# Two layers of attention and a feed-forward: projections dealt out into the leads, and loads asked in another order

## The chip, the cores and the metric

One NeuronCore of one Trainium2 chip. The metric is the device time of one execution in microseconds (us), the median of several runs. Five engines work side by side, each through its own instructions in order, and wait for each other by counting semaphores: TensorE (PE in the profile; PEld is its weight loads) multiplies from SBUF into the eight banks of PSUM; ScalarE (ACT) and VectorE (DVE) read PSUM and SBUF; GpSimd (POOL) works on SBUF; SyncE (SP) issues most of the DMA transfers. An engine that waits keeps everything behind it in its own queue waiting, the DMAs that it is to issue included.

## The reference

All in float32. `x` is (2, 512, 320), `ctx` is (2, 1024, 192).

```
# layer 0: 8 heads of 40
enc, ca = ctx[:, :-4], ctx[:, -4:]
hs   = mha(x @ Wq, enc @ Wk, enc @ Wv)                  # 512 queries, 1020 keys
q1   = einsum('btc,th->bch', ca, Wq_ca)[:, indices]     # 192 rows, repeated to 512
hs1  = mha(q1, x, x)                                    # 512 keys
hs2  = mha(hs1 @ Wq, ca @ Wk_ca, ca @ Wv_ca)            # 4 keys
x    = (hs + hs2) @ Wout + b_out + x
# layer 1: 20 heads of 16
h1 = ln(x); x = attn(h1, h1,  q1, k1, v1, o1_w, o1_b) + x   # self: 512 keys
h2 = ln(x); x = attn(h2, ctx, q2, k2, v2, o2_w, o2_b) + x   # cross: 1024 keys
h3 = ln(x); a, g = split(h3 @ ff_w1 + ff_b1)
out = (a * gelu(g)) @ ff_w2 + ff_b2 + x
```

## The kernel before, in words

**Numbers.** Matmuls run on a reduced-precision float type (fp32r). Where float32 is wanted, an operand is split into a high part (a cast by ScalarE) and a low part (the difference, by VectorE, in join phases by GpSimd), and a product is the sum of high by high, high by low and low by high. A feature tile is 128, 128 or 64 of the 320 features (`FTILES`), held on partitions. Of the last tile both parts share 128 partitions ("mixed"). The class `Prepared` (L407) holds these splits of inputs: `first_in` for the first layer, `self_in`, `cross_in` for the second; its semaphore `low` counts the parts in a fixed order.

**Projections** (`Projection`, L466) are lists of jobs. A job of kind "s" makes one feature tile of queries or keys: a group of matmuls into one of a few PSUM banks, ScalarE's copy into the high half of one of four slots of the tile `split` (the ring), VectorE's subtraction into the low half, SyncE's store of both to a DRAM scratch (`q0_d`, `k0_d`, `q1_d`, ...). A slot may be filled again when its store has landed (semaphores `stored`); a bank when VectorE is done with it (`low`). A job of kind "v" makes the values of 128 tokens: five or eight matmuls of 320 columns into one of two banks, copied by ScalarE. Kinds "k" and "w" make small products for the image tokens (`ca`), with small matmuls. `first` (L506) has the queries and keys of batch 0 and the values of both batches of layer 0; `second` (L507) the rest of layer 0 and the keys and values of cross attention; `selfp` and `selfv` the queries and keys, and the values, of self attention; `crossp` the queries of cross attention.

**Attention** (`Stream`, `Attention`). A group is two heads (layer 0) or four (layer 1) of a batch. SyncE loads a group's keys and queries from the scratch into one of four slots (`k_sl`, `q_sl`; `sp_load` L706: four DMAs a group in layer 0, eight in layer 1). Each group is passed twice. In the first pass ("items", `item` L805) TensorE makes scores with queries on partitions, 512 keys an item, into the banks 4, 5 and 6 in turn, and VectorE takes each item's maximum (`reduce` L966, line L974, one instruction an item). When a group is done (`part_maxima` L949), its negated maxima are split in two parts, turned by TensorE (`flip` L820), copied by ScalarE (`flipped`) and sent by a DMA into two more rows of the queries (`sp_load_m` L696). In the second pass the scores come out with keys on partitions and the maximum already subtracted (`scores` L841), ScalarE takes the exponential (L938), and `values` (L857) multiplies by the values into bank 7.
Items are counted in chunks: two items a chunk in layer 0, four in layer 1, one chunk per step of the second pass. The first pass runs ahead of the second by `lead` chunks: 13 in the first attention, 8 in self, 12 in cross. So each attention opens with a lead in which there is only the first pass; then steps of both. `first` attention and cross attention have two items per row of scores (1020 and 1024 keys), self has one. In the first attention's lead the jobs of `second` are dealt out over the 13 chunks by count (`share` L510), after the items of each chunk; `probs`, where the exponentials go, lies on the ring, so ScalarE waits for all stores before the first exponential.

**The front.** SyncE issues the loads "a" (x of batch 0, Wq), "c" (context of batch 0, Wk, Wv), "e" (context of batch 1). GpSimd clears some tiles and, when the nine low parts of `first` are done, issues "d" (weights of the image tokens, Wout, a mask) and "f" (x of batch 1, k2, v2, the identity, small tensors): eleven DMAs. The engines run `first`, split the remaining inputs, and start the first attention. SyncE loads group 0's slot after all stores of `first`, group 1's and 2's in the lead after the shares 0 and 4.

**Between the attentions** lie joins (`pe_join` L1205, `dve_join` L1251, `act_join` L1280): per token tile the output projection, residual, layer norm, a transpose, the split of the result. `early` (L1200) puts the first half of the next projection's jobs behind the last three token tiles, and the rest behind the join. Then come (self) `selfv`, the wait for all low parts, and the lead; (cross) the wait for all low parts, and the lead. In `sp_self` (L759) group 0 is loaded after eight stores and when six have landed; in `sp_cross` (L780) keys are loaded ahead, and the queries of group 0 after three stores have landed.

The feed-forward ends the kernel.

## Time and profile before

| | us |
|---|---|
| median of 3 runs (910.27 to 910.87) | 910.78 |
| profiled execution | 911.72 |
| its span | 909.9 |
| TensorE busy | 842.4 (93%) |
| VectorE busy | 605.4 (67%) |
| ScalarE busy | 474.5 (52%) |
| GpSimd busy | 101.7 (11%) |

A busy TensorE is not one at its peak: its granted clock is a column of its own in the windows (1.00 is 2.4 GHz, 0.50 is 1.2 GHz). The chain that ended last is 62% TensorE and 23% VectorE. All times of rows are microseconds from the start of the span.

### The profile page before, as it was taken

The numbers are of one execution on the slowest core, as the hardware profiler recorded it, in microseconds if no ns is written. First come the engines' busy times: TensorE is split into PE (matmuls) and PEld (weight loads), VectorE is DVE, ScalarE is ACT, GpSimd is POOL, SyncE is SP. The second block draws the span as 40 slices with busy tenths as digits, with TensorE's granted clock in tenths as the row PEclk, the third lists the DMA queues.
The fourth block names the chain that finished last, engine by engine and source line by source line (L and its number), as shares of the span: only waits on it lengthen the run. The fifth ranks groups of instructions, "written<-read, shape, count | busy, mean of one in ns | idle before, by whom it ended". The sixth has DMA issues, their size and how long they took to land.

```text
span 909.9 us, 11416 instructions
## 1 busy us (share of the span) xinstructions
PE 842.4 (93%) x4148; PEld 461.6 (51%) x4148; DVE 605.4 (67%) x1147; ACT 474.5 (52%) x706; POOL 101.7 (11%) x142
## 2 busy tenths in 40 slices
PE   4759989999999999999998989999999999899998
PEld 3647644444457577433333643333333332578988
DVE  4245547777685343889994688999999991866241
ACT  4523344545543352366677704776766779575030
POOL 3200000500004142000001610000000000130000
PEclk9968999999997999589999956999999999999999
DMA  6938658733212047122207230222232000600000
GB/s 222 275 104 239 205 155 282 199 85 110 65 57 66 1 134 222 59 71 68 66 11 128 71 127 1 54 54 54 53 54 53 1 1 2 246 0 1 30 1 30
DMA packets 30967, 83.18 MB, mean 91 GB/s; under 512 B 5173, under 2 KB 9213, under 8 KB 28607
## 3 DMA queue, kind: packets, MB, share of 16 engines
q1 hardware_dynamic: 30110, 79.71, 30.9%
q0 software_dynamic: 800, 2.73, 1.0%
q8 instruction: 33, 0.54, 0.3%
q14 instruction: 24, 0.19, 0.1%
HBM read 56.12 MB, written 25.89 MB: 90 GB/s over the span
## 4 chain that ended last, share of the span: by engine, by line
PE 62%; DVE 23%; DMA 7%; ACT 3%; issue 3%; POOL 1%; SPq 0%; ACTq 0%; DVEq 0%; POOLq 0%
PE PS L872 17%; PE PS L815 13%; DVE maxp L974 10%; PE PS L1408 8%; PE PS L566 7%; PE PS L852 6%; DVE negm L974 5%; PE PS L1426 4%; PE PS L1213 3%; DMA k_d<-split 2%; DMA ca_nat<-in_ca 2%; DVE turned L1007 1%; DMA q_sl<-msplit 1%; ACT probs L938 1%; DMA w_v<-in_Wv 1%
## 5 line engine op out<-in xcount | busy, mean ns | idle before, releaser
L938 ACT ACTIVATE probs<-PS 128x1024 f32<-128x1024 f32 (+1 forms) x336 | 311.7, 972 | 149.9 <-PE PS L852 144.4
L974 DVE TENSOR_REDUCE maxp<-PS 128x1 f32<-128x512 f32 x448 | 280.1, 679 | 44.6 <-PE PS L815 43.6
L815 PE MATMUL PS<-k_sl,q_sl 48*128 48x512 f32 (+3 forms) x640 | 262.4, 489 | 24.1 <-DMA q_sl<-q_d 11.2
L815 PEld LDWEIGHTS PS<-k_sl,q_sl 48*128 48x128 f32 (+2 forms) x640 | 119.3, 199 | 200.8 <-DVE maxp L974 120.5
L852 PE MATMUL PS<-q_sl,k_sl 50*128 50x512 f32 (+3 forms) x672 | 203.2, 433 | 8.3 <-ACT probs L938 5.2
L974 DVE TENSOR_REDUCE negm<-PS 128x1 f32<-128x512 f32 (+1 forms) x192 | 120.9, 679 | 29.4 <-PE PS L815 29.3
L852 PEld LDWEIGHTS PS<-q_sl,k_sl 50*128 50x128 f32 (+2 forms) x672 | 102.7, 191 | 56.0 <-ACT probs L938 24.4
L872 PE MATMUL PS<-probs,v2c 128*32 128x512 f32 x640 | 86.6, 610 | 1.0
L604 DVE TENSOR_TENSOR split<-PS,split 128x512 fp32r<-128x512 f32 (+3 forms) x54 | 34.9, 650 | 53.7 <-ACT split L581 53.7
L872 PE MATMUL PS<-probs,v0c 128*64 128x512 f32 (+1 forms) x256 | 62.8, 612 | 0.0
L581 ACT CAST split<-PS 128x512 fp32r<-128x512 f32 (+3 forms) x54 | 29.8, 554 | 52.8 <-PE PS L566 41.4
L1039 POOL TENSOR_TENSOR packed<-turned,recip 128x256 f32<-128x256 f32 x20 | 12.7, 635 | 372.2 <-DVE recip L1010 372.2
L1408 PE MATMUL PS<-act_high,w_high 128*128 128x512 f32 x120 | 48.0, 400 | 3.8 <-DVE w_low L1384 2.5
L1007 DVE STREAM_TRANSPOSE turned<-PS 128x512 f32<-128x512 f32 (+1 forms) x36 | 22.9, 637 | 40.6 <-PE PS L872 40.0
L872 PE MATMUL PS<-probs,v1c 128*32 128x512 f32 x320 | 45.6, 639 | 2.1 <-DVE turned L1007 1.2
L1408 PE MATMUL PS<-act_high,w_low 128*128 128x512 f32 x120 | 47.3, 394 | 0.0
L922 ACT CAST msplit<-PS 32x128 fp32r<-32x128 f32 (+2 forms) x36 | 9.0, 249 | 72.6 <-PE PS L826 72.6
L1285 ACT ACTIVATE act_t<-PS,params 128x128 f32<-128x128 f32 x72 | 27.8, 457 | 17.3 <-PE PS L1231 17.3
L1408 PE MATMUL PS<-act_low,w_high 128*128 128x512 f32 x80 | 31.6, 396 | 0.0
L566 PE MATMUL PS<-x_high,w_q_high 128*128 128x512 f32 (+1 forms) x42 | 14.8, 449 | 17.1 <-DVE w_s_low L427 12.2
L872 PEld LDWEIGHTS PS<-probs,v0c 128*64 128x64 f32 (+1 forms) x256 | 15.7, 138 | 28.6 <-issue 25.6
L1469 DVE SCALAR_TENSOR_TENSOR ff_raw<-PS,params,gelu 128x512 f32<-128x512 f32 x20 | 15.0, 750 | 20.8 <-ACT gelu L1449 20.8
(182 smaller groups left out, 1012.8 us busy)
## 6 DMA issues: line engine op xcount, KB each, us to landing
k_d<-split SPq DMA_DIRECT2D x20, 512.0 KB, 3.6
q_d<-split SPq DMA_DIRECT2D x12, 512.0 KB, 3.1
k_sl<-k_d SPq DMA_DIRECT2D x8, 640.0 KB
k_sl<-k_d SPq DMA_DIRECT2D x40, 128.0 KB
q_sl<-q_d SPq DMA_DIRECT2D x40, 128.0 KB
k_sl<-k_d SPq DMA_DIRECT2D x20, 256.0 KB
w_raw<-in_ff_w SPq DMA_DIRECT2D x1, 3840.0 KB, 11.6
k_d<-split SPq DMA_DIRECT2D x10, 256.0 KB, 3.4
```

The costliest lines, as they stand in the source:

```text
L566: mm = nc.tensor.matmul(o, w, a, start=(k == 0), stop=(k == len(j["mm"]) - 1))
L581: nc.scalar.copy(split[0:j["m"], i % RING, 0, 0:j["n"]], split_bank(ph, j)).then_inc(ph.high, 1)
L604: nc.vector.tensor_tensor(split[0:j["m"], i % RING, 1, 0:j["n"]], split_bank(ph, j), split[0:j["m"], i % RING, 0, 0:j["n"]].bitcast(F32), ...
L815: nc.tensor.matmul(PS[0:a.qt, SBANKS[k % 3], 0:cn], q_view(g)[f:f + a.rows, j // a.stack, q * a.qt:(q + 1) * a.qt], k_view(g)[f:f + a.rows ...
L852: mm = nc.tensor.matmul(PS[0:sz, 2 * (x % 2) + half, 0:a.nq], k_view(g)[f:f + a.rows + 2, j // a.stack, t * 128:t * 128 + sz], q_view(g)[f ...
L872: mm = nc.tensor.matmul(PS[w * j:w * j + w, OBANK, 0:a.nq], a.vc[0:sz, tile, a.vw * h:a.vw * h + w], probs[0:sz, x % PRING, half, 0:a.nq], ...
L938: nc.scalar.activation(probs[0:a.size[t], x % PRING, :, 0:a.nq], PS[0:a.size[t], 2 * (x % 2):2 * (x % 2) + 2, 0:a.nq], ACT.Exp, scale=a.sc ...
L974: nc.vector.tensor_reduce((maxp if nch > 1 else negm)[0:a.qt, g.turn, o:o + 1], PS[0:a.qt, SBANKS[k % 3], 0:a.chunks[c][1]], AX.X, ALU.max ...
L1007: nc.vector.transpose(turned[:, 0:a.nq], PS[:, OBANK, 0:a.nq]).then_inc(st.out_read, 1)
L1285: o = nc.scalar.activation(act_t[0:fn, m, t * 128:(t + 1) * 128], PS[0:fn, 4 + t % 2, 128 * m:128 * m + 128], ACT.Identity, bias=params[0: ...
L1408: mm = nc.tensor.matmul(PS[:, up_bank(i, part), :], w[:, k, f0:f0 + 128], a[:, k, cols], start=(n == 0), stop=(n == len(UP_TERMS) - 1))
L1426: mm = nc.tensor.matmul(PS[:, 4 + t % 4, 0:D], a[:, m, rows], w[:, m, :], start=(m == 0 and n == 0), stop=(m == FT - 1 and n == 2))
```

## The change

1. **The front.** "a" is split: x has its own semaphore and Wq ("q") another, so that x is cast when it is there. x and the context are split by feature tiles (`x0a`, `x0b`, `c1a`, ...). Keys are made tile by tile (both halves of the 1024 keys of a tile in turn), and ScalarE and VectorE split the context of batch 1 between key jobs. The values of batch 1 go from `first` to `second`. `second` begins with the keys of batch 1; its jobs name the inputs that they need, and the splits of x of batch 1, k2 and v2 stand in front of single jobs; the small products of the image tokens are dealt out among the others. Group 0's slot load is issued after seven stores, when five have landed. GpSimd issues x of batch 1 when "c" has landed, and "f" and "d" when group 0's slot has been loaded.
2. **Self attention.** After the join only the first six jobs of `selfp` are made; the other six and the eight of `selfv` are dealt out over seven of the lead's eight chunks. In both leads with jobs, a chunk's jobs now stand before its items. `selfp` has three banks. Slot loads stand between the stores.
3. **Cross attention.** In the lead a chunk's four items go to banks 0 to 3 or 4 to 7, and VectorE takes all four maxima in one instruction. The queries of group 0 are loaded after one store.

The diff, cut to its core:

```diff
     loads = {
-        "a": [(act_t[:, :, 0:SQ], ins["x_t"][:, :, 0:SQ]), (w_s0[:], ins["Wq"])],
+        "a": [(act_t[:, :, 0:SQ], ins["x_t"][:, :, 0:SQ])],
+        "q": [(w_s0[:], ins["Wq"])],
...
+        "x": [(act_t[:, :, SQ:TOK], ins["x_t"][:, :, SQ:TOK])],
+        "f": [(w_k2[:], ins["k2"]), (w_v2[:], ins["v2"]),
...
     def first_jobs():
-        return q0_jobs(0) + key_jobs(WK0, k0_d, 0) + value_jobs(WV0, 0, v0c, 0) + value_jobs(WV0, 0, v0c, 1)
+        return q0_jobs(0) + key_jobs(WK0, k0_d, 0) + value_jobs(WV0, 0, v0c, 0)
 
     def second_jobs():
+        q_jobs, k_jobs = q0_jobs(1), key_jobs(WK0, k0_d, 1)
+        k_jobs[0]["needs"] = ("c1a", "c1b")
+        k_jobs[2].update(prepare=("x1a",), prepare_loaded=(loaded_x1, ALL_X1))
+        k_jobs[4].update(prepare=("x1b",), prepare_loaded=(loaded_x1, ALL_X1))
+        q_jobs[0]["needs"] = ("x1a", "x1b")
+        q_jobs[0].update(prepare=("wk2",), prepare_loaded=(loaded_f, ALL_F))
+        q_jobs[1].update(prepare=("wv2",), prepare_loaded=(loaded_f, ALL_F))
...
+        ca_jobs[0]["loaded"] = (loaded_f, ALL_F)
...
+        split_jobs = k_jobs + q_jobs
+        for i, j in enumerate(k2_jobs):
+            split_jobs += [j] if i % 2 == 0 else [j, ca_jobs[i // 2]]
...
+        ca_rows[0]["loaded"] = (loaded_d, ALL_D)
...
+        whole_jobs = value_jobs(WV0, 0, v0c, 1) + v2_jobs[:2] + ca_rows[:1] + v2_jobs[2:4] + ca_rows[1:]
+        whole_jobs += v2_jobs[4:9] + ca_outs[:1] + v2_jobs[9:12] + ca_outs[1:] + v2_jobs[12:]
...
     first = Projection("first", first_jobs())
-    second = Projection("second", second_jobs(), (0, 1, 2), (3, OBANK))
-    selfp = Projection("selfp", self_jobs(), (2, 3, 6, 7))
+    second = Projection("second", second_jobs(), (0, 1, 2), (3, OBANK), first)
+    selfp = Projection("selfp", self_jobs(), (2, 3, OBANK))
...
+    class Side:
...
+        def share(self, x):
+
+            n = len(self.jobs)
+            return self.jobs[min(x, self.span) * n // self.span:min(x + 1, self.span) * n // self.span]
+
+    def alternate(ph, jobs, other, others):
+
+        out = []
+        for i, j in enumerate(jobs):
+            out += [(ph, j)] + ([(other, others[i // 2])] if i % 2 else [])
+        return out + [(other, j) for j in others[len(jobs) // 2:]]
+
+    first_side = Side([(second, j) for j in second.jobs], A_MAIN.lead)
+    self_side = Side(alternate(selfp, selfp.jobs[2 * KF:], selfv, selfv.jobs), A_SELF.lead - 1)
...
     def sp_first(sp):
         st = S_FIRST
-        first.wait_stored(sp)
+        sp_projection(sp, first, first.jobs[:Q0_END + 4])
         sp.wait_ge(first_ones, 1)
+        first.wait_some_stored(sp, Q0_END + 2)
         sp_load(sp, st, 0)
+        sp_projection(sp, first, first.jobs[Q0_END + 4:])
         for x in range(A_MAIN.kt + 1):
-            sp_projection(sp, second, share(second, x, st.lead))
+            sp_projection(sp, second, [j for _, j in first_side.share(x)])
+            if x == 0:
+                first.wait_stored(sp)
             if x in (0, 4):
                 sp_load(sp, st, 1 + x // 4)
...
     def sp_self(sp):
         st = S_SELF
-        sp_projection(sp, selfp, selfp.jobs[:2 * KF + 2])
+        sp_projection(sp, selfp, selfp.jobs[:4])
         sp.wait_ge(stack_ones, 1)
-        selfp.wait_some_stored(sp, 2 * KF)
+        selfp.wait_some_stored(sp, 2)
         sp_load(sp, st, 0)
-        sp_projection(sp, selfp, selfp.jobs[2 * KF + 2:])
-        for i in range(1, SLOTS - 1):
-            sp_load(sp, st, i)
+        sp_projection(sp, selfp, selfp.jobs[4:2 * KF])
+        sp_load(sp, st, 1)
+        sp_projection(sp, selfp, selfp.jobs[2 * KF:2 * KF + 4])
+        selfp.wait_some_stored(sp, 4)
+        sp_load(sp, st, 2)
+        sp_projection(sp, selfp, selfp.jobs[2 * KF + 4:])
+        sp_load_m(sp, st, 0)
+        selfp.wait_stored(sp)
         sp.dma_start(w_s0[:], ins["q2"]).then_inc(loaded_q2, 16)
...
     def sp_cross(sp):
...
-        sp_projection(sp, crossp, crossp.jobs[:KF])
+        sp_projection(sp, crossp, crossp.jobs[:1])
+        crossp.wait_some_stored(sp, 1)
+        sp_load_q(sp, st.groups[0])
+        sp_projection(sp, crossp, crossp.jobs[1:KF])
...
+        def wide_items(c):
+            per = st.groups[0].a.per_step
+            if c >= 2:
+                pe.wait_ge(st.score_free, per * (c - 1))
+            for n, (i, m) in enumerate(st.chunk(c)[1]):
...
+                nc.tensor.matmul(PS[0:a.qt, wide_bank(c) + n, 0:cn],
...
+            if st.chunk(c)[0] is not None:
+                pe.wait_ge(st.score_free, per * c)
+                flip(st.chunk(c)[0], waits=False)
...
         for x in range(st.lead):
-            maxima([x])
-            if side is not None:
-                pe_projection(pe, side, share(side, x, st.lead))
-            flips([x])
...
+            if wide:
+                wide_items(x)
+            else:
+                if side is not None:
+                    for ph, j in side.share(x):
+                        pe_projection(pe, ph, [j])
+                maxima([x])
+                flips([x])
+        if wide:
+            pe.wait_ge(st.score_free, st.groups[0].a.per_step * (st.lead - 1 + st.lead % 2))
...
+        def wide_maxima(c):
...
+            dve.wait_ge(st.score, st.item_at[i, m] + a.per_step)
+            to = maxp[0:a.qt, g.turn, :].rearrange("p (e r c) -> p r c e", e=a.stack, c=2)[:, t, :, :]
+            nc.vector.tensor_reduce(to, PS[0:a.qt, wide_bank(c):wide_bank(c) + 4, :].rearrange(
+                "p (c e) n -> p c e n", e=a.stack), AX.X, ALU.max).then_inc(st.score_free, a.per_step)
...
@@ VectorE's program @@
-            first_in.dve(dve, "c0", "wk0", "wv0")
-            dve_projection(dve, first, first.jobs[:K0_END])
+            first_in.dve(dve, "c0a", "c0b", "wk0", "wv0")
+            dve_projection(dve, first, first.jobs[:Q0_END + 3])
             dve.wait_ge(loaded_e, ALL_E)
-            first_in.dve(dve, "c1")
+            first_in.dve(dve, "c1a")
+            dve_projection(dve, first, first.jobs[Q0_END + 3:Q0_END + 5])
+            first_in.dve(dve, "c1b")
+            dve_projection(dve, first, first.jobs[Q0_END + 5:K0_END])
             dve.wait_ge(loaded_f, ALL_F)
-            first_in.dve(dve, "x1", "wk2", "wv2")
             dve.wait_ge(loaded_d, ALL_D)
-            dve_attention(dve, S_FIRST, side=second)
+            dve_attention(dve, S_FIRST, side=first_side)
@@ GpSimd's program @@
             pool_rows_first(pool, range(SLOTS - 1), 1)
-            pool.wait_ge(first.low, first.ns)
+            pool.wait_ge(loaded_c, ALL_C)
+            for dst, part in loads["x"]:
+                pool.dma_start(dst, part).then_inc(loaded_x1, 16)
+            pool.wait_ge(q_loaded[S_FIRST.groups[0].place], S_FIRST.groups[0].loads)
+            for dst, part in loads["f"]:
+                pool.dma_start(dst, part).then_inc(loaded_f, 16)
             for dst, part in loads["d"]:
                 pool.dma_start(dst, part).then_inc(loaded_d, 16)
-            for dst, part in loads["f"]:
-                pool.dma_start(dst, part).then_inc(loaded_f, 16)
```

## Rows read from the trace of the kernel before

**Rows 1.** Windows of 10 us: stretch, length, busy of each engine, clock, DMA, GB/s.
```profile
40.00:50.00 10.00, 2.08 (x14) 1.70 (x12) 0.00 (x0) 1.77 (x8) 0.00 (x0) 0.80 0.71 205
...
530.00:540.00 10.00, 10.00 (x18) 4.78 (x17) 10.00 (x18) 0.00 (x0) 0.00 (x0) 0.50 0.32 100
```

**Rows 2.** Chain that ended last, in order of time: start, us, what.
```profile
35.60 15.41 DMA ca_nat<-in_ca
```

**Rows 3.** Timeline of TensorE, front: start, us, line, operands, count, [idle before <-releaser].
```profile
32.37 0.42 PE L566 MATMUL PS<-w_v_high,ctx_high 128*128 128x320 f32 x1
...
33.95 0.42 PE L566 MATMUL PS<-w_v_high,ctx_high 128*128 128x320 f32 x1
...
51.42 1.19 PE L815 MATMUL PS<-k_sl,q_sl 120*128 120x512 f32 x2 [9.35 <-DMA q_sl<-q_d]
56.19 1.65 PE L566 MATMUL PS<-x_high,w_q_high 128*128 128x512 f32 x3 [3.58 <-DVE w_v_low L427]
...
118.21 0.31 PE L566 MATMUL PS<-w_v_low,ctx_high 128*128 128x320 f32 x1
```

**Rows 4.** Timeline of ScalarE and VectorE, front and end of the first lead.
```profile
27.88 0.58 ACT L581 CAST split<-PS 64x512 fp32r<-64x512 f32 x1 [0.97 <-DMA k_d<-split]
...
52.62 1.23 DVE L427 TENSOR_TENSOR act_low<-act_t,x_high 128x1024 fp32r<-128x1024 f32 x1 [19.70 <-ACT x_high L420]
...
122.32 2.87 ACT L938 ACTIVATE probs<-PS 128x1024 f32<-128x1024 f32 x3 [3.34 <-DMA k_d<-split]
```

**Rows 5.** Timeline of DMA issues by SyncE and GpSimd, front.
```profile
33.24 0.95 SPq L692 DMA_DIRECT2D k_sl<-k_d  x1
...
29.83 0.74 POOL L1601 DMA_DIRECT2D w_kca<-in_Wk_ca  x1 [22.05 <-DVE split L604]
```

**Rows 6.** DMA issues of the whole span: queue, count, KB each, us to landing.
```profile
w_s<-in_Wout POOLq DMA_DIRECT2D x1, 480.0 KB, 5.3
```

**Rows 7.** DMA of the stretch 56 to 123.
```profile
DMA packets 6787, 13.16 MB, mean 196 GB/s; under 512 B 542, under 2 KB 1822, under 8 KB 6544
...
q_d<-split SPq DMA_DIRECT2D x1, 256.0 KB, 9.9
```

**Rows 8.** Half-microsecond windows of TensorE alone: length, busy, clock, DMA, GB/s.
```profile
83.50:84.00 0.50, 0.50 (x3) 0.56 0.95 284
```

**Rows 9.** Timelines of TensorE, SyncE, VectorE and ScalarE, self attention's lead.
```profile
337.27 0.39 PE L566 MATMUL PS<-x_high,w_s_low 128*64 128x512 f32 x1
...
335.03 0.36 SPq L617 DMA_DIRECT2D k_d<-split  x1
...
359.07 9.66 DVE L974 TENSOR_REDUCE negm<-PS 128x1 f32<-128x512 f32 x16 [9.12 <-PE PS L815]
...
378.61 3.85 ACT L938 ACTIVATE probs<-PS 128x1024 f32<-128x1024 f32 x4 [6.10 <-PE PS L852]
...
389.79 1.94 ACT L938 ACTIVATE probs<-PS 128x1024 f32<-128x1024 f32 x2 [2.32 <-PE PS L852]
```

**Rows 10.** Windows of 2 us, self attention, all engines.
```profile
394.00:396.00 2.00, 2.00 (x14) 0.68 (x14) 2.00 (x4) 1.89 (x2) 0.00 (x0) 0.96 0.38 109
```

**Rows 11.** Timelines of TensorE, VectorE and ScalarE, cross attention's lead.
```profile
526.56 0.70 PE L815 MATMUL PS<-k_sl,q_sl 48*128 48x512 f32 x3 [1.84 <-DMA q_sl<-q_d]
...
525.37 0.68 DVE L604 TENSOR_TENSOR split<-PS,split 64x512 fp32r<-64x512 f32 x1 [1.14 <-ACT split L581]
527.06 19.23 DVE L974 TENSOR_REDUCE maxp<-PS 128x1 f32<-128x512 f32 x32 [1.01 <-PE PS L815]
546.32 0.19 DVE L957 TENSOR_REDUCE negm<-maxp 128x16 f32<-128x32 f32 x1
...
556.39 3.85 ACT L938 ACTIVATE probs<-PS 128x1024 f32<-128x1024 f32 x4 [6.10 <-PE PS L852]
...
564.86 1.94 ACT L938 ACTIVATE probs<-PS 128x1024 f32<-128x1024 f32 x2 [0.77 <-PE PS L852]
567.56 1.94 ACT L938 ACTIVATE probs<-PS 128x1024 f32<-128x1024 f32 x2 [0.77 <-PE PS L852]
```

226 lines of the change are left out of this document (139 added, 87 removed).

## The prediction

> **What bounds the kernel now.** I read the ten-microsecond windows first, then the chain of waits, then the timeline of each engine around the places where TensorE stands still. TensorE is near 10 us busy in almost every ten, so only the exceptions count: 2.08 us between 40 and 50, and the leads of the two later attentions, where VectorE is at 10.00 of 10 and the granted clock at 0.50 [rows 1]. Three places:
>
> - Front. TensorE starts nothing between the end of the first phase (42.1) and 51.42, then two scores, then the second phase at 56.19 [rows 3]. The chain puts 15.41 us on the last of GpSimd's eleven bulk loads [rows 2]; ScalarE and VectorE sit until it lands, VectorE for 19.70 us [rows 4]. The second phase runs TensorE full from 56.19 to 118.5 [rows 3]; the first exponential follows at 122.32, held by the last store [rows 4].
> - Self attention's lead. All projections and values are made first; then VectorE reduces 32 score tiles back to back from 359.07, and the first exponential comes at 378.61 [rows 9]. The clock, lost in this lead, is back at 394 to 396 [rows 10].
> - Cross attention's lead: 48 reductions from 527.06, first exponential 556.39 [rows 11].
>
> The attention loops between these places are not edited; they should shift as blocks.
>
> **Part 1, the front.** Nothing of the second phase needs the bulk loads at once any more: it opens with keys of the second batch. TensorE's first phase loses eight value jobs; two of them take 1.58 us [rows 3], 0.79 each, so 6.3 us. They come back in the second phase. The first phase ends about 32.5: 42.1 less 6.3, less some 3 from the earlier start (x no longer waits for Wq) and from ScalarE taking the key copies in smaller turns. By itself this would let the second phase start 24 us earlier.
>
> But one wait stays: VectorE still waits for all of f and d before it enters the first attention's lead, and these loads are now issued later. GpSimd waits for the slot load of group 0. That load is issued after five stores have landed. ScalarE's last key copy at 27.88 was waiting for the fifth store [rows 4]; with the start 1.9 us earlier and some of it lost in VectorE's queue I take 26.5 instead of 33.24 [rows 5]. It moves 1.44 MB behind 1 MB of stores. In the stretch from 56 to 123 the queues moved 196 GB/s on the mean [rows 7], with peaks of 300; at 260 this is 9.5 us, so 36 (33 to 39; the row of before, issued at 33.24 against the bulk loads, ended at 51.4). Behind it GpSimd issues ten loads, where eleven took 6.3 us [rows 5, 2], so the last begins 5.2 us later, and lands 5.3 us after that, as the Wout load did [rows 6]. VectorE is let go at 46.5: 41 with the slot load at 33 and 3 us to land, about what ScalarE waited for a store in [rows 4]; 52 with 39 and 8.
>
> Queued behind that wait are the low parts of the key jobs, and for them TensorE's three split banks. TensorE gets three key jobs (512 columns where a value job streams 320, so 1.2 us each), three value jobs and two scores done, 6.3 us in all, and stands from about 39 to 47.2. So the earlier start of the first phase and the lighter first phase are worth nothing: what decides is the landing of d.
>
> Work of the second phase: 56.19 to 118.5 is 62.3 us; 3.5 us at its start and 9.7 after 83.5 [rows 8] ran at half clock and half of each is loss (6.6), 0.5 was idle, leaving 55.2. Plus 6.3 of values moved in, less 6.3 done ahead: 55.2 from 47.2. I add 1.75 for 3.5 us at half clock after the stand, as at 56, and 1.5 for stores that wait behind the slot load of group 1 (one store took 9.9 us so [rows 7]). I add nothing for a second fall of the clock: the one at 83.5 came after the run of short 4-row products of the image queries, which are now dealt out among key jobs; its price is 4.9. TensorE ends at 105.7. From the last value product to the first exponential it took 3.8 us, set by the last store; two value jobs follow the last split job now instead of one, so 3.0. First exponential 108.7 instead of 122.32: **-13.6**. Ends: -8 (VectorE free at 52, or the stores twice as late) and -19 (free at 41). The x load of the second batch, now issued by GpSimd near 12, lies where the queues are a third busy; it costs nothing, and 2 to 3 us if the context load lands later for it.
>
> **Part 2, self attention's lead.** Six of twelve split jobs stay in the join; SyncE's fourth store is issued at 335.03 [rows 9], so group 0's slot load (eight issues at 0.6 behind it) lands near 342.5. TensorE ends the sixth job at 337.5 [rows 9] (the product that starts at 337.27 is its last), two more make 341.1, and it waits 1.4 for the first scores. After that come 12 jobs (four split jobs at 1.85, eight value jobs at 1.17: 16.8 us) and 32 scores (7.5). Where a chunk's last job is a split job, VectorE does its low part before the reductions, and the fourth score waits for the first reduction: copy 0.6, low 0.7, reduction 0.65, so 1.5 us of stall, at three chunks; at the other five about 0.4. 342.5 + 16.8 + 7.5 + 6.5 of stalls + 1.6 for the last reduction, the scores and the hand-over: the first exponential at 374.9 instead of 378.61: **-3.7**. In the old order TensorE worked from 337.5 to 357.8 and VectorE from 359.07 to 378.6; laid fully beside each other the limit is -12 (no stalls), and 0 if each chunk stalls twice as long. Late next: group 3's load, now issued near 374 after GpSimd's memset, needed near 387.
>
> The clock: before, the steps from 378.61 to 389.79 took 11.2 us for three [rows 9]; at full clock 2.7 each [rows 11] and about one 0.5 for the change of group. Up to 395 this makes 4.2 us. In the new lead TensorE is busy about four fifths of the time, and in the second phase it held at such density; I take it that the clock holds: **-4.2**. If it falls, this is 0 and some of the lead runs at half, +2 to +8.
>
> **Part 3, cross attention.** The rows of group 0 are asked for after one store, not three; but TensorE also waits for all six low parts, and the last ends at 526.05 [rows 11], while its first score started at 526.56. Gain 0.5, not the 4 us that the request is earlier. Then 48 reductions become 12 over four banks. From 32 to 512 elements a reduction grows from 0.19 to 0.68 [rows 11], 1.03 ns an element, so 2048 take 2.27, about 2.2 from start to start; four singles take 2.40 (19.23 over 32). The refill of four banks at half clock (three times 0.43, plus 0.79 and the hand-overs) is as long, so I take 2.3. First reduction at 527.3 (four scores, not one, ahead of it), eleven of 2.3, 0.55 for the group's parts, 1.2 for the scores: 554.4 instead of 556.4: **-2.0**. Ends: -3.2 at 2.19, +2.7 at 2.73 (no overlap at all).
>
> The Trainium skill (VectorE: DVE Perf Modes, the section on the TRN2 errata) gives a fixed 120 cycles to each instruction that reads PSUM. By it three such terms per chunk would go, 0.375 us each chunk, -4.5 over the lead, if VectorE alone set the pace. The starts above, 0.60 apart where its formula gives 0.66, say that part of the fixed time is already overlapped.
>
> **Sum.** -13.6 - 3.7 - 4.2 - 2.0 = -23.5, from the profiled execution of 911.72 (span 909.9): 888.2. The median of the runs shown stands 0.94 below that execution: **887.3**.
>
> **Rivals.**
> A. Self attention's clock falls again: its 4.2 is gone and a few us of work run at half, about +6: 893. For it: the clock fell at 83.5 after half a microsecond of idling [rows 8]; against it: the work is dense, full-row.
> B. The loads land by 41 or earlier, and VectorE's wait is nearly covered: 880. For it: nothing but stores competes; against it: ten issues cannot be shortened.
> C. Slot loads and stores collide: 12.8 MB must now move in 59 us, not 63. Two stalls of 4 us and one fall of the clock (4.9), less the 1.5 charged: about +9, 897 with a little from A.
> D. The other side: the clock does not come back. In the leads TensorE would stand a short while at every chunk for VectorE, which now stands behind copies. Each us of work at half clock costs one. Half of the front's 55 us at half gives +27.6, and with self attention's 4.2 gone it is 919. It decides from 24 us of such work on. For it: the cross lead stayed at 0.50 for ten windows long at this kind of pace [rows 1]; against it: there TensorE worked 40% of the time, here 80. The Trainium skill (TensorE: Matmul & The Clock Gate, "A second HAM failure mode: psum-queue depth-cycling") names this very pattern, micro-idling between groups of products that cycle through banks. By it D, or A, would be the outcome; this trace shows both, the lead that stayed low and loops over rotating banks that ran at 1.00 after it [rows 10].
> E. It doesn't do what it says: d lands so late (70, not 46.5) that VectorE's wait eats everything: about 911. Nothing in the rows moves it so far.
>
> **Chances.** Forecast 0.43, A 0.22, B 0.13, C 0.15, D 0.05, E 0.02. The forecast's own range is 882 to 892; with A to C and the ends above 878 to 899, leaving out 2 in 10. A difference under 0.2% (1.8 us) can't be told from none. Faster 0.93, same 0.02, slower 0.05.
>
> **What would show it.** Right: VectorE idle from about 28 to 46 ended by a d load, TensorE idle 39 to 47, first exponentials near 109, 361 and 531 (each shifted by what went before), no 0.50 window in self attention's lead, 12 reductions 2.2 to 2.3 apart. Wrong: if TensorE never stands before 100, B; if windows of 0.50 lie across a lead, A or D; if ScalarE waits on stores for more than 5 us, C; if the wide reduction takes over 2.7 us, part 3 turns.

## The result and the profile after

The changed kernel took **897.59 us** (median of 4 runs, 897.33 to 902.52) against 910.83 in runs beside it: ratio **0.9875** (95% interval 0.9839 to 0.9911). Run again on another chip it took 894.71 against 910.31 there: 0.9826 (0.9806 to 0.9846). The forecast was 887.3: right in sign and 10 us too good. The time lies outside the forecast's own range (882 to 892) and inside the wide one with the rivals (878 to 899), at the 897 of rival C. The profiled execution took 897.33 (span 895.5), 14.4 less than the one before.

Places at which the work passes the same point, in the two traces (us; a low part is VectorE's subtraction of a split job):

| place | before | after | gained so far | forecast |
|---|---|---|---|---|
| first attention, first exponential | 122.32 | 112.94 | 9.4 | 13.6 |
| first join, first output product | 293.5 | 282.2 | 11.3 | 13.6 |
| its first low part for self attention | 328.81 | 316.69 | 12.1 | 13.6 |
| self attention, first exponential | 378.61 | 366.60 | 12.0 | 17.3 |
| second join, first low part | 514.07 | 500.59 | 13.5 | 21.5 |
| cross attention, first exponential | 556.39 | 539.28 | 17.1 | 23.5 |
| third join, first standard deviation | 777.77 | 762.04 | 15.7 | 23.5 |
| feed-forward, first gelu | 802.29 | 787.85 | 14.4 | 23.5 |

The front after, from the timelines of all engines (start, length, line, what, [idle before <-releaser]); the lines answer to [rows 3 to 5]:

```profile
26.67 0.94 SPq L747 DMA_DIRECT2D k_sl<-k_d  x1
...
39.93 1.22 PE L915 MATMUL PS<-k_sl,q_sl 120*128 120x512 f32 x2 [2.70 <-DMA q_sl<-q_d]
40.19 0.59 POOL L1735 DMA_DIRECT2D w_k<-in_k  x1 [26.20 <-DMA q_sl<-q_d]
...
45.00 0.54 POOL L1737 DMA_DIRECT2D hmask<-in_hmask  x1
49.53 1.29 DVE L659 TENSOR_TENSOR split<-PS,split 128x512 fp32r<-128x512 f32 x2 [20.73 <-DMA hmask<-in_hmask]
50.28 0.79 PE L617 MATMUL PS<-ctx_high,w_k_high 128*128 128x512 f32 x1 [6.19 <-DVE split L659]
...
65.48 0.59 ACT L634 CAST split<-PS 128x512 fp32r<-128x512 f32 x1 [6.17 <-DMA k_d<-split]
67.99 0.41 PE L617 MATMUL PS<-w_v_high,ctx_high 128*128 128x320 f32 x1 [1.90 <-ACT v0c L647]
...
87.28 0.58 ACT L634 CAST split<-PS 64x512 fp32r<-64x512 f32 x1 [4.49 <-DMA cq_d<-split]
...
112.94 3.80 ACT L1046 ACTIVATE probs<-PS 128x1024 f32<-128x1024 f32 x4 [1.80 <-DMA cq_d<-split]
```

Group 0's slot load leaves at 26.67 (forecast 26.5) and lands at 39.9 (36). Over these 13.26 us the queues moved 211 GB/s, 2.8 MB (window: length, busy of TensorE, its weight loads, VectorE, ScalarE, GpSimd, then clock, DMA share, GB/s):

```profile
26.67:39.93 13.26, 9.52 (x55) 8.10 (x53) 2.07 (x3) 7.39 (x24) 0.00 (x0) 1.00 0.78 211
```

Only when the slot load has landed does GpSimd issue f and d; VectorE, idle for 20.73 us, starts at 49.53 (46.5), TensorE at 50.28 (47.2). Two waits of ScalarE for stores follow, 6.17 and 4.49 us, each ending 13 to 14 us behind the issue of a slot load (51.40, 73.79), and TensorE idles for 1.90 and 1.19. A third idling, 0.81 at 92.4, ends with VectorE's split of the maxima, not with a store.

Self attention's lead after, TensorE and ScalarE, beside [rows 9]:

```profile
330.36 0.73 PE L915 MATMUL PS<-k_sl,q_sl 48*128 48x512 f32 x3 [1.15 <-DMA q_sl<-q_d]
331.65 0.50 PE L915 MATMUL PS<-k_sl,q_sl 48*128 48x512 f32 x1 [0.56 <-DVE negm L1082]
...
337.35 0.50 PE L915 MATMUL PS<-k_sl,q_sl 48*128 48x512 f32 x1 [1.34 <-DVE negm L1082]
...
361.62 3.07 PE L915 MATMUL PS<-k_sl,q_sl 48*128 48x512 f32 x5 [0.55 <-DVE negm L1082]
364.23 1.32 PE L952 MATMUL PS<-q_sl,k_sl 50*128 50x512 f32 x4
365.30 1.28 ACT L1046 ACT_TABLE_LOAD   x1 [4.42 <-PE PS L952]
366.60 3.85 ACT L1046 ACTIVATE probs<-PS 128x1024 f32<-128x1024 f32 x4
```

Each fourth score waits for VectorE (seven stands of 0.55 to 1.34, 5.4 in all). At the end stands something that the old order hid: ScalarE loads the exponential's table at 365.30, when the scores are there, for 1.28 us. In the kernel before the same load ran right behind ScalarE's last copy, and the wait for the scores (6.10 us) came after it:

```profile
371.23 1.28 ACT L938 ACT_TABLE_LOAD   x1
```

e4, with the old order, has it early as well (load at 357.95, exponential at 365.33), and so has cross attention in the changed kernel (532.62 and 539.28). What differs in the program is that the new order makes ScalarE wait for all stores of the projections just ahead of this exponential. That these further waits are what puts the load behind the scores' wait is argued, not tried alone.

The clock of TensorE in windows of 5 us (the last three columns are granted clock, DMA share, GB/s):

```profile
355.00:360.00 5.00, 4.45 (x27) 3.58 (x27) 2.48 (x4) 1.28 (x3) 0.00 (x0) 1.00 0.31 102
360.00:365.00 5.00, 4.06 (x15) 1.99 (x14) 4.12 (x7) 0.43 (x1) 3.60 (x2) 0.92 0.00 0
365.00:370.00 5.00, 2.88 (x14) 1.20 (x15) 2.17 (x6) 4.68 (x5) 0.00 (x0) 0.50 0.55 157
...
375.00:380.00 5.00, 5.00 (x28) 1.91 (x22) 3.27 (x6) 2.39 (x3) 0.00 (x0) 0.72 0.04 9
```

In this execution it stayed at 1.00 through the lead's stands, fell near 364, 2.4 us before the first exponential, and was back near 378. Cross attention's lead, TensorE, VectorE and ScalarE, beside [rows 11]:

```profile
512.60 1.19 PE L892 MATMUL PS<-k_sl,q_sl 48*128 48x512 f32 x8 [1.39 <-DVE split L659]
513.48 11.08 DVE L1096 TENSOR_REDUCE maxp<-PS 128x4 f32<-128x2048 f32 x5 [0.93 <-PE PS L892]
515.82 1.22 PE L892 MATMUL PS<-k_sl,q_sl 48*128 48x512 f32 x4 [2.03 <-DVE maxp L1096]
518.02 1.22 PE L892 MATMUL PS<-k_sl,q_sl 48*128 48x512 f32 x4 [0.98 <-DVE maxp L1096]
...
539.28 3.85 ACT L1046 ACTIVATE probs<-PS 128x1024 f32<-128x1024 f32 x4 [5.38 <-PE PS L952]
```

Five wide reductions in a row take 11.08 us, 2.20 from start to start; TensorE makes four tiles in 1.22 and then waits 0.98 for VectorE.

### The profile page after: what moved, and what is told of

Same layout as the page of the kernel before. It is cut to its first block, busy times and chain, and to the rows that moved or that the text cites. A ratio compares the mean times of both kernels' runs of the same rounds, so it can differ in the third digit from the quotient of the medians.

```text
span 895.5 us, 11401 instructions
## 1 busy us (share of the span) xinstructions
PE 816.9 (91%) x4148; PEld 449.4 (50%) x4148; DVE 602.3 (67%) x1111; ACT 473.8 (53%) x708; POOL 101.5 (11%) x142
## 4 chain that ended last, share of the span: by engine, by line
PE 59%; DVE 22%; DMA 8%; issue 4%; ACT 4%; SPq 2%; POOL 1%; ACTq 0%; DVEq 0%; POOLq 0%
PE PS L972 17%; PE PS L915 12%; PE PS L1536 8%; DVE maxp L1082 8%; PE PS L952 6%; PE PS L617 6%; DVE negm L1082 5%; PE PS L1554 4%; DMA k_d<-split 3%; PE PS L1338 3%; DVE maxp L1096 2%; DMA q_sl<-q_d 1%; DVE turned L1128 1%; DMA q_sl<-msplit 1%; ACT probs L1046 1%
## 5 line engine op out<-in xcount | busy, mean ns | idle before, releaser
L1082 DVE TENSOR_REDUCE maxp<-PS 128x1 f32<-128x512 f32 (+1 forms) x400 | 251.0, 678 | 42.3 <-PE PS L915 41.3
L915 PE MATMUL PS<-k_sl,q_sl 48*128 48x512 f32 (+2 forms) x592 | 225.7, 451 | 18.7 <-DVE negm L1082 5.4
L915 PEld LDWEIGHTS PS<-k_sl,q_sl 48*128 48x128 f32 (+2 forms) x592 | 102.2, 188 | 175.9 <-DVE maxp L1082 105.2
L659 DVE TENSOR_TENSOR split<-PS,split 128x512 fp32r<-128x512 f32 (+3 forms) x54 | 34.7, 649 | 70.2 <-ACT split L634 49.4
L1507 ACT CAST ff_high<-ff_raw 128x512 fp32r<-128x512 f32 x20 | 12.4, 622 | 30.9 <-DVE ff_raw L1597 30.7
```

Source lines behind the costliest of these rows:

```text
L659: nc.vector.tensor_tensor(split[0:j["m"], ph.slot(i), 1, 0:j["n"]], split_bank(ph, j), split[0:j["m"], ph.slot(i), 0, 0:j["n"]].bitcast(F3 ...
L915: nc.tensor.matmul(PS[0:a.qt, SBANKS[k % 3], 0:cn], q_view(g)[f:f + a.rows, j // a.stack, q * a.qt:(q + 1) * a.qt], k_view(g)[f:f + a.rows ...
L1082: nc.vector.tensor_reduce((maxp if nch > 1 else negm)[0:a.qt, g.turn, o:o + 1], PS[0:a.qt, SBANKS[k % 3], 0:a.chunks[c][1]], AX.X, ALU.max ...
```

## Experiments

Fourteen runs, all from the changed kernel and timed beside the kernel before, where single times of one kernel spread over 2 to 12 us. So the verdicts rest on places in the traces, one trace a run. "Lead" is from the join's first low part to the first exponential. An asterisk marks the place that the edit aims at.

| run | median | ratio (95%) | 1st exp. | self lead | cross lead |
|---|---|---|---|---|---|
| changed, first | 897.59 | 0.9875 (0.9839-0.9911) | 112.9 | 49.9 | 38.7 |
| changed, again (e11) | 894.71 | 0.9826 (0.9806-0.9846) | 112.5 | 49.7 | 38.7 |
| e1 VectorE let go | 895.88 | 0.9852 (0.9794-0.9911) | 109.2* | 52.3 | 38.7 |
| e2 loads early | 889.96 | 0.9791 (0.9734-0.9848) | 104.6* | 49.3 | 38.7 |
| e3 slot loads by GpSimd | 906.46 | 0.9956 (0.9927-0.9985) | 118.6* | 49.4 | 38.7 |
| e4 part 1 alone | 899.96 | 0.9896 (0.9859-0.9932) | 111.6 | 49.8* | 42.3* |
| e5 table ahead | 898.08 | 0.9883 (0.9806-0.9961) | 114.5 | 51.0* | 38.7 |
| e6 fourth score moved | 895.39 | 0.9848 (0.9799-0.9896) | 113.0 | 47.4* | 38.7 |
| e7 d loads late | 894.08 | 0.9797 (0.9725-0.9870) | 106.8* | 52.4 | 38.7 |
| e8 single reductions | 901.92 | 0.9907 (0.9873-0.9941) | 112.6 | 49.8 | 41.9* |
| e9 two and two | 895.75 | 0.9840 (0.9818-0.9863) | 112.9 | 46.5* | 38.7 |
| e10 e2 and e9 | 888.24 | 0.9753 (0.9727-0.9780) | 106.5 | 47.1* | 38.7 |
| e12 over eight chunks | 891.89 | 0.9786 (0.9755-0.9818) | 105.8 | 50.6* | 38.7 |
| e13 no slot bytes | 897.82 | 0.9857 (0.9809-0.9904) | 111.6* | 52.6 | 38.7 |
| e14 final | 885.35 | 0.9716 (0.9680-0.9751) | 106.9 | 43.0* | 38.7 |

What a place is worth can be read from the runs that leave its stretch alone. Seven profiles have the changed front (changed, e11, e4, e5, e6, e8, e9): first exponential 111.6 to 114.5. Four have e2's front (e2, e10, e12, e14): 104.6 to 106.9. Nine have the changed kernel's order in self attention's lead: 49.3 to 49.9 in five of them (changed, e11, e2, e3, e8), 51.0 to 52.6 in the four in which TensorE's clock fell inside the lead (e1, e5, e7, e13). Cross attention's lead is 38.7 in all thirteen that have it whole.

**e1.** What is VectorE's wait worth?
```diff
-            dve.wait_ge(loaded_f, ALL_F)
-            dve.wait_ge(loaded_d, ALL_D)
```


> The changed kernel, but VectorE no longer waits for the f and d loads before the first attention's lead (TensorE's own wait orders what reads them). Theory L (the landing of the last bulk load decides, as the forecast had it): VectorE starts the low parts of the key jobs at about 28, TensorE goes on at 41.2, after the slot load of group 0, instead of 50.28 after 6.19 us of idling; 9 us earlier, and 1.9 us more if the half clock of 50 to 54 goes with the stand. First exponential 102 to 104 instead of 112.94, the whole 886 to 888. Theory S (slot loads and stores share the queues, and the store ring of four decides as soon as VectorE does not): the stores of the first eight jobs now leave while the ten bulk loads are still landing, ScalarE's waits for stores grow from 6.2 and 4.5 to over 15 in all; first exponential 107 to 110, the whole 892 to 895.

```profile
60.09 0.59 ACT L634 CAST split<-PS 128x512 fp32r<-128x512 f32 x1 [10.76 <-DMA k_d<-split]
62.60 0.63 PE L617 MATMUL PS<-w_v_high,ctx_high 128*128 128x320 f32 x1 [6.51 <-ACT v0c L647]
...
109.18 2.92 ACT L1046 ACTIVATE probs<-PS 128x1024 f32<-128x1024 f32 x3 [1.80 <-DMA cq_d<-split]
```
TensorE goes on at 39.44 behind the slot load and has no stand at 50. But it stands 6.51 us before 62.6, since ScalarE waits 10.76 for a store: 3.8 gained of 9. Stores issued at 44.6 to 48.8, behind the late bulk loads, took 13.7 to 16.2 us. This is theory S: the stand was moved, and the landing of d was not the last limit.

**e2.** f and d not held back: `pool.wait_ge(q_loaded[...])` ahead of them taken out.

> The changed kernel, with GpSimd issuing the ten f and d loads at once after the x loads (near 14), not after the slot load of group 0. VectorE keeps its wait. If holding the loads back is what costs: they land by 34, VectorE is free before the slot load of group 0, and TensorE stands only for that slot load; first exponential 104 to 107, the whole 889 to 892. If the loads crowd the stores and the slot load of group 0 (1.44 MB, 13.2 us now), the slot load lands at 46 to 50 instead of 39.9 and the gain is 0 to 3: first exponential 110 to 113.

```profile
26.78 0.44 PE L617 MATMUL PS<-ctx_high,w_k_high 128*64 128x512 f32 x1 [2.80 <-DVE split L659]
42.42 0.74 PE L915 MATMUL PS<-k_sl,q_sl 120*128 120x512 f32 x2 [2.03 <-DMA q_sl<-q_d]
...
104.55 3.82 ACT L1046 ACTIVATE probs<-PS 128x1024 f32<-128x1024 f32 x4 [1.81 <-DMA cq_d<-split]
```
The early stores are crowded (TensorE idle 2.80 at 26.8), and the slot load is issued 3.8 later (30.47) and lands 2.5 later. But VectorE never waits for a load, and the stands of TensorE near 50 and 68 are gone: 8.4 us earlier, and 6.0 to 7.1 in the three later runs with this front. Holding the bulk loads back is what the front lost.

**e3.** Slot loads of groups 1 and 2 in GpSimd's queue.
```diff
-            if x in (0, 4):
-                sp_load(sp, st, 1 + x // 4)
...
+            first.wait_stored(pool)
+            sp_load(pool, S_FIRST, 1)
+            sp_load(pool, S_FIRST, 2)
             sp_load_m(pool, S_FIRST, 0)
```


> The changed kernel, with the slot loads of groups 1 and 2 issued by GpSimd behind the f and d loads (about 46 to 54) instead of by SyncE between stores of the second phase. If the stores wait behind the slot loads in SyncE's queue (rival C's mechanism), ScalarE's waits of 6.17 (near 65) and 4.49 (near 87) go, and with them the 3.9 us that TensorE idles between 54 and 94: first exponential 109, the whole 893.5. If only the bytes matter, not the queue, the waits stay but move to 55 to 62, and the first exponential stays within 1 us of 112.9. VectorE's release at 49.5 stays in both.

```profile
51.37 0.80 PE L617 MATMUL PS<-ctx_high,w_k_high 128*128 128x512 f32 x1 [8.77 <-DVE split L659]
65.29 0.58 ACT L634 CAST split<-PS 64x512 fp32r<-64x512 f32 x1 [9.03 <-DMA k_d<-split]
66.30 0.58 PE L617 MATMUL PS<-w_v_high,ctx_high 128*128 128x320 f32 x1 [4.04 <-ACT v0c L647]
```
Neither came true: the wait near 87 went, the one near 65 grew to 9.03, TensorE stood 8.77 and 4.04, and the clock fell twice more (near 66 and 80). The first exponential is 5.7 us later. The stores that SyncE issued at 51.4 to 55.5 took 13.0 to 14.7 us, though the slot loads stood in another queue: that queue does not keep them apart. The edit also brings both slot loads at once, so its loss is not the price of the queue alone.

**e13.** The same transfers without their bytes. SyncE's slot loads of groups 1 and 2 become four issues of 2.5 KB each, and GpSimd fills these slots with constants, so the kernel leaves out part of the first attention.

> The changed kernel without the bytes of two slot loads: groups 1 and 2 of the first attention are not brought in, four issues of 2.5 KB each stand in their place and the slots are filled with constants, which leaves out part of the computation; every other transfer, wait and instruction of the front stays. GpSimd's filling delays the x loads of the second batch by some 9 us. If the slot loads' 1.44 MB each are what the stores wait behind, the waits of 6.2 (near 65) and 4.5 (near 87) go, TensorE does not idle between 54 and 94, and the first exponential comes at 109 (112.9 less 3.9). If the wait near 65 is mainly the end of the f and d loads, it stays at 4 or more and only the one near 87 goes: 111.5.

```profile
51.70 0.79 PE L617 MATMUL PS<-ctx_high,w_k_high 128*128 128x512 f32 x1 [6.09 <-DVE split L659]
...
111.64 3.80 ACT L1056 ACTIVATE probs<-PS 128x1024 f32<-128x1024 f32 x4 [1.81 <-DMA cq_d<-split]
```
Between these lines ScalarE has no wait for a store of 0.5 us or more. Stores issued at 55 to 61 land in 2.8 to 3.7 us, where those at the same point of the changed kernel took 9.2 to 11.2. From TensorE's restart to the first exponential it is 59.9 us instead of 62.7 (62.2 to 62.8 in the runs with this front in which the clock did not fall again); the 1.4 later restart hides half of it in the total. The slot loads' bytes make the store waits, worth 2.7 (3.9 was expected; the idling of 0.8 for VectorE was in that, and stays with 0.7).

**e7.** Half of the loads early: f at once, d behind the slot load, VectorE free.

> The changed kernel, but the five f loads issued at once (near 14), the five d loads still behind the slot load of group 0, and VectorE waiting for neither. Issuing all ten early moved the first exponential from 112.94 to 104.55, while the early stores were crowded (a ScalarE wait of 5.4, TensorE idle 2.8 near 26); letting VectorE go alone moved it to 109.18, with 10.8 us of store wait near 60 behind the late loads. If the bytes in flight decide, half of them early and half late gives the early stores back 1 to 2 us and costs 2 to 3 near 60: first exponential 104 to 106, the whole 888 to 891. If the collision near 60 comes mainly from the d loads (1.18 MB of the 1.9), it is 107 to 109, as with VectorE let go alone. If holding back the d loads is harmless once nothing waits for them, 102 to 103.5.

106.79, with a store wait of 7.26 near 56 and TensorE idle 3.00: between the first two guesses. It lies among the four runs with all ten loads early (104.6 to 106.9), so that holding back the d loads costs anything, once VectorE waits for neither, is not shown.

**e4.** Parts 2 and 3 undone (the second attention's order, single reductions and late rows as before).

> Part 1 alone: the front as changed, but self attention's projections, values and order, and cross attention's single reductions and late rows, as before. If the parts add, the first exponentials are at 112.9 (as changed), at 378.6 less 12 = 366.5 for self attention (the same 366.6 as with part 2, since the new lead took 49.9 us from the join's first low part where the old took 49.8), and cross attention's 3.5 later than with part 3. The clock after self attention's first exponential should be back at 382, as before (16 us after it), where part 2 has it back 11 us after: that is worth 1 to 2. The whole: 897.3 + 1.5 + 2.3 to 3.5 = 901 to 903. If part 2's lead was in fact worth the forecast 3.7 and something else ate it, self attention's first exponential comes at 370.

```profile
315.53 0.69 DVE L658 TENSOR_TENSOR split<-PS,split 128x512 fp32r<-128x512 f32 x1
...
365.33 3.85 ACT L1037 ACTIVATE probs<-PS 128x1024 f32<-128x1024 f32 x4 [6.10 <-PE PS L943]
```
The parts add. Self attention's lead is 49.8 in the old order and 49.9 in the new: part 2 gave nothing there. Nor in the loop: from its first exponential to the next join's first low part it is 134.0 in both (135.5 before). But e2, e3 and e9, which all have part 1 and jobs in the lead, took 135.4 to 135.5, as the kernel before. So the 1.5 belongs to where the clock comes back in an execution, and is not shown to come from the change. Cross attention's lead is 3.6 longer without part 3.

**e8.** Single reductions, early rows.

> The changed kernel with cross attention's 48 single reductions in place of 12 wide ones; the rows of its first groups still asked for early. Time from the join's first low part (500.59 in the changed kernel) to the first exponential: 38.7 there, 42.3 before and with part 1 alone. If, as forecast, the rows asked early are worth 0.5, it is 41.8; if TensorE's wait for the last low part decides alone, 42.3, and the wide reductions carry all of the 3.6 (0.3 a chunk). The whole 897.3 + 3.1 to 3.6.

41.9: rows asked early 0.4, wide reductions 3.2.

**e5.** One exponential ahead of the wait.
```diff
+        if st is S_SELF:
+            nc.scalar.activation(ahead[:, 0:1], eps[:, :], ACT.Exp)
```


> The changed kernel with one more ScalarE instruction: an exponential of one column before ScalarE's wait for the first scores of self attention, so that the exponential table is loaded ahead of that wait. In the changed kernel the load (1.28 us) starts at 365.30, when the scores are there, and the first exponential follows at 366.60. If it is on the path, the first exponential comes 49.9 - 1.3 = 48.6 us after the join's first low part (316.69 there), and the whole is 1.3 less, 896.0. Rival: the scores run at half clock there anyway and TensorE is the next to be waited for; then the distance stays at 49.9.

```profile
367.36 1.28 ACT L1041 ACT_TABLE_LOAD   x1
368.66 0.20 ACT L1041 ACTIVATE ahead<-eps 128x1 f32<-128x1 f32 x1
371.25 3.85 ACT L1049 ACTIVATE probs<-PS 128x1024 f32<-128x1024 f32 x4 [2.39 <-PE PS L953]
```
The load now ends 2.6 us before the exponential, so it is off the path; but in this execution the clock had fallen inside the lead (0.66 from 340 to 345, 0.68 from 355 to 360) and the distance is 51.0. The total does not show the gain. The other three leads of this order with falls at the same two points (e1, e7, e13) took 52.3 to 52.6, so 1.3 to 1.6 more: the size of the line's 1.28.

**e6.** Three scores, the next chunk's jobs, the fourth score.

> The table edit, and another order in self attention's lead: of each chunk's four score tiles three are made, then the next chunk's two projection or value jobs, then the fourth, so that TensorE no longer stands for the first reduction (six stands of 0.55 to 1.34, 4.86 in all after the first chunk). Theory of the stalls: the distance from the first low part to the first exponential falls from 49.9 to 43.8 (4.86 of stands and 1.28 of the table load), the whole to 891. Rival: the slot load of group 1 (issued 341.8 to 347 in the changed kernel, needed at the fifth chunk, then at 351.6, now wanted at 347) is late next, and gives back 2 to 3: distance 46 to 47, the whole 893.5 to 894.5.

Five of the seven stands stayed (1.34, 0.55, 1.33, 0.55, 0.55): four scores still followed each other over three banks, one place further on. The lead lost 2.5 us, 1.28 of it the table and 1.1 the two stands that went; the edit missed its aim.

**e9.** Job, two scores, job, two scores (VectorE in the same order).
```diff
-                for ph, j in side.share(x):
-                    pe_projection(pe, ph, [j])
-                maxima([x])
+                jobs = side.share(x)
+                for ph, j in jobs[:1]:
+                    pe_projection(pe, ph, [j])
+                maxima([x], 0, 2)
+                for ph, j in jobs[1:]:
+                    pe_projection(pe, ph, [j])
+                maxima([x], 2)
```


> The table edit, and each chunk of self attention's lead as job, two scores, job, two scores, in TensorE's and VectorE's order. Moving the fourth score behind the next chunk's jobs had left the stands of 1.34, 0.55, 1.33, 0.55: four scores still followed one another over three banks, and the last of them waited as before. Theory of the banks: with never more than two in a row the six stands (4.86 us) go; from the first low part to the first exponential 49.9 - 4.86 - 1.28 = 43.8, the whole 890.5 to 891.5. Rival one, group 1's slot load is late next (issued 341.8 to 347 in the changed kernel): 46 to 47. Rival two, the stands are the time of VectorE in disguise (32 reductions of 0.62 and six low parts of 0.69 are 24 of the 36 us): then shortening TensorE's stands just moves the wait to the last chunk, and the distance is over 47.

```profile
330.35 0.80 PE L916 MATMUL PS<-k_sl,q_sl 48*128 48x512 f32 x2 [3.57 <-DMA q_sl<-q_d]
...
360.62 1.69 PE L916 MATMUL PS<-k_sl,q_sl 48*128 48x512 f32 x3 [0.55 <-DVE negm L1089]
...
362.58 3.85 ACT L1053 ACTIVATE probs<-PS 128x1024 f32<-128x1024 f32 x4 [1.20 <-PE PS L953]
```
All stands but the last 0.55 are gone. The lead is 3.4 shorter, not 6.1 (rival one came close in size, 46 to 47, but it was group 0's load that was late, not group 1's): with one job ahead of the first scores, not two, they now wait 3.57 for group 0's slot load. From that landing to the first exponential it is 32.2, where it was 36.2.

**e10, e11, e12.**

> All ten bulk loads issued at once, the table edit, and job, two scores, job, two scores in self attention's lead. If the two places add: first exponential near 104.6 (8.4 earlier than in the changed kernel), self attention's another 6.1 earlier, so 366.6 - 8.4 - 6.1 = 352; the whole 897.3 - 8.4 - 6.1 = 883, with 3 either way for where the clock falls. If the gain of the lead is as small as with the fourth score moved (2.5), 886.5.

> The changed kernel once more, unedited, to see what a single profile of it is worth. If the places where the clock falls are a lottery, this profile differs from the first in the lead of self attention, in its loop or in the last join by 1 to 3 us each, and the first exponential stays within 1 of 112.9. If they are fixed by the program, each stretch agrees within 0.3.

> As the one with early loads and job, two scores, job, two scores, but with the fourteen jobs of self attention's lead over all eight chunks, not seven, so that the last chunk's scores stand beside a job. In the changed kernel the last chunk (five scores from 361.62, the first exponential's scores at 364.23) runs at VectorE's pace, about 1.5 us slower than TensorE's. If that is the wait, the lead is another 1 to 1.5 shorter; if the last value copy now stands between, or the jobs moved back leave stands in other chunks, it is the same or 0.5 longer.

e10 has both edits: 888.24, where 883 was expected, or 886.5 with a small gain of the lead. Its first exponential came at 106.5, not 104.6, and its lead again waits for the slot load, 3.02 us. e12 missed: chunks with one job left have four scores in a row (a stand of 1.62), the clock was low in parts of the lead, and the table load came back close to the path, behind the last value copy. e11 is the same program as the changed kernel; its leads agree within 0.2, but look at the third join (windows, the changed kernel first, then e11):

```profile
775.00:780.00 5.00, 2.58 (x8) 1.98 (x9) 4.86 (x11) 1.93 (x6) 1.93 (x2) 0.72 0.86 313
780.00:785.00 5.00, 5.00 (x18) 3.90 (x17) 1.19 (x3) 1.88 (x4) 4.36 (x6) 0.60 0.04 18
```
```profile
775.00:780.00 5.00, 2.17 (x11) 1.59 (x11) 4.89 (x9) 2.46 (x7) 2.46 (x2) 1.00 0.75 266
780.00:785.00 5.00, 3.51 (x19) 2.66 (x18) 2.68 (x5) 3.73 (x8) 3.82 (x4) 1.00 0.16 65
```
From the first standard deviation to the first gelu it is 25.8 us in the first execution and 23.0 in e11. The first two stretches of that guess, self attention's lead and its loop, agree within 0.3.

**e14.** e10 with both jobs of the first chunk ahead of its scores.

> All ten bulk loads early, the table edit, and the lead of self attention as job, two scores, job, two scores, but with both jobs of the first chunk ahead of its scores, as in the changed kernel. With one job ahead, the slot load of group 0 came 3.57 and 3.02 late where it had been 1.15 late, which ate 2 us. If that was the rest of the wait, the distance from the first low part to the first exponential is 46.5 or 47.1 less 1.9 = 44.6 to 45.2 (49.9 in the changed kernel), and the whole 883 to 887 in the median; if TensorE's work there is fixed by the later slot loads, it stays at 46.5.

```profile
322.41 0.73 PE L916 MATMUL PS<-k_sl,q_sl 48*128 48x512 f32 x3 [1.26 <-DMA q_sl<-q_d]
...
349.72 1.69 PE L916 MATMUL PS<-k_sl,q_sl 48*128 48x512 f32 x3 [0.55 <-DVE negm L1089]
...
351.69 3.85 ACT L1053 ACTIVATE probs<-PS 128x1024 f32<-128x1024 f32 x4 [1.19 <-PE PS L953]
```
43.0, better than expected: the slot load is waited for 1.26. **885.35** (881.73 to 888.25), ratio 0.9716 (0.9680 to 0.9751): faster than before and, by ratios on different chips, 1.1 to 1.6% faster than the changed kernel.

## Why the prediction was right in sign and wrong in size

Forecast -23.5, profile to profile -14.4. Three steps failed. The front's slot load was taken at 9.5 us and took 13.2, and the waits behind it were charged 1.5 and came to 3.9. Self attention's lead was to gain 3.7 by overlap and gained nothing. Its clock was to hold past the first exponential and fell 2.4 us before it. Cross attention's lead gave 1.6 more than forecast.

- **Front: -9.4, not -13.6.** The slot load was sized as 2.4 MB at 260 GB/s; the trace has 2.8 MB at 211. It lands 3.9 late, the loads behind it make up 0.8, and TensorE restarts 3.1 late. TensorE's idling after the restart was charged 1.5 and came to 3.9, of which 3.1 are store waits (rival C's mechanism, without its fall of the clock); the end was 1.2 better. 3.1 + 2.4 - 1.2 = 4.3. The work after the restart was right: 62.7 less 3.9 of idling, 1.6 lost at half clock and 1.8 at the end is 55.3, forecast 55.2. "What decides is the landing of d" was half true: freed of it (e1), the next limit stood 3.8 us further on. What these runs share is bytes in flight: e13 shows it for the store waits, by removing the bytes, and e2 moves bytes to where less else ran. That x of batch 1, issued at 13.04, costs nothing was not tried alone.
- **Self attention's lead: 0, not -3.7.** From the first score to the first exponential 32.4 were forecast and 36.2 measured. The stands were charged 6.5 and were 5.4. Missed were the table load (1.28), and the last chunk, which has no job beside it: five tiles from 361.62 take 3.07 at VectorE's pace, where 0.93 was charged for the tiles and 0.4 of stall. The twelve jobs, read from start to start in TensorE's timeline, took 17.9 and not 16.8. This leaves some 0.8 us unplaced. e14, with all but two of the stands and the table load off the path, is 6.9 under the changed kernel's lead, so the overlap was there to be had.
- **Self attention's clock: -1.5, not -4.2.** The forecast let the clock hold through the lead and beyond. In the changed kernel's two executions it held to the last 3 us of the lead and was then at half from about 364 to 378 (before: 363 to 394), so the steps of the loop were not spared. The 1.5 is not shown to be the change's, as e4 against e2, e3 and e9 says. The Trainium skill (TensorE: Matmul & The Clock Gate, "A second HAM failure mode: psum-queue depth-cycling") expects throttling where TensorE idles briefly between groups over cycling banks. The traces agree in part: of the nine leads with seven such stands, the clock fell twice inside four (e1, e5, e7, e13; 0.66 to 0.69 over five us each time) and not before the last 4 us in five. What decides between them stays open.
- **Cross attention: -3.6, not -2.0.** The early rows gave 0.4 (forecast 0.5). A wide reduction starts every 2.20, not 2.3: VectorE alone sets the pace and TensorE's refill is hidden, since TensorE waits 0.98 for it. The Trainium skill's fixed cost of an instruction that reads PSUM (VectorE: DVE Perf Modes, TRN2 errata) would make -4.5; measured for the reductions, -3.2.
- **Not forecast:** 2.7 gained between the first exponential and the second lead, and 2.7 given back behind the cross lead, 1.4 in its loop and 1.3 in the last join. In the kernel before the clock fell near 125 and stayed low for 14 us in the first join; in this execution of the changed kernel it did not fall near 125 and was low there for 10. Over all sixteen profiles the first of these stretches took 201.7 to 206.5 us, cross attention's loop 221.3 to 228.7 and the last join 23.0 to 25.8, and e11, the same program as the changed kernel, has 203.8, 224.0 and 23.0. One profile a kernel can't give any of these to the change. What the runs support is the front, 9.4 (7.8 to 10.8 over the seven profiles that have it), and the cross lead, 3.6; their sum is near the 13.2 between the medians.

On the rivals: D did not happen. A's fall came, at the end of the lead, and took most of the 4.2, but not the further microseconds at half inside the lead. C's sign came true (ScalarE waited 6.17 for a store), at about a third of its price: its two stalls cost 3.1, not 8, and the fall of its clock did not come in this execution. So the total at C's 897 is chance: it is the sum of the misses above. C's own sum was wrong too: 8 + 4.9 - 1.5 is 11.4, not 9. And the end "0 if each chunk stalls twice as long" adds 6.5 to -3.7, which is +2.8.

## What to carry to other kernels

A load held back to clear the queues must land somewhere; price the place where it lands, not only the one that it leaves, and look first whether it can go earlier. When VectorE's wait or any cover is moved, list what the old order hid at the same place (here a table load of 1.28 us) and what the next waiter is after it. In a lead that mixes jobs and score tiles, do not put more tiles in a row than there are banks: four over three banks stood every time, two in a row did not; three with a job behind them was not tried. And take a second profile of the same program before a difference of 1 to 3 us in a long stretch is explained.

## What was not expected of the hardware

- The same program on another execution had its clock at 1.00 where it had been at 0.72 and 0.60 for ten microseconds, a difference of 2.8 us; in the fifteen profiles of the changed kernel and its variants self attention's loop, which no edit touches, took 131.7 to 136.9. Where TensorE's clock falls over such a stretch can't be put down to a small edit from one profile.
- The exponential's table load ran 1.28 us and the exponential followed 1.30 after its start. The Trainium skill (ScalarE: Activation LUTs, "What ACT_TABLE_LOAD costs") gives 1283 ns for the load, which agrees, and a further 1.38 us for a drain. That does not show here, nor where ScalarE worked right up to the load: in the kernel before three activations end at 800.98, and load and gelu follow at once.

```profile
799.82 1.16 ACT L1285 ACTIVATE act_t<-PS,params 128x128 f32<-128x128 f32 x3 [0.30 <-PE PS L1231]
801.00 1.28 ACT L1449 ACT_TABLE_LOAD   x1
802.29 0.69 ACT L1449 ACTIVATE gelu<-PS,params 128x512 f32<-128x512 f32 x1
```

- Slot loads issued by GpSimd (e3) landed 7.7 to 16.3 us after issue. SyncE's key stores of 512 KB took 8.9 us in the median from 10 to 70 us, against 4.0 in the changed kernel, and the ones just behind the slot loads 13.0 to 14.7. DMA issues of e3 in that stretch, queue, count, KB each, median us to landing:

```profile
k_d<-split SPq DMA_DIRECT2D x8, 512.0 KB, 8.9
...
k_sl<-k_d POOLq DMA_DIRECT2D x2, 640.0 KB, 10.6
...
q_sl<-q_d POOLq DMA_DIRECT2D x2, 160.0 KB, 14.8
```
